# Projections of q and k as f32r products of high and low parts, in place of fp32 products, in an attention and experts kernel

## What is computed

```python
q = _split_heads(x @ Wq.T + bq); k = _split_heads(x @ Wk.T + bk); v = _split_heads(x @ Wv.T + bv)
q = jnp.exp(q); k = jnp.exp(k)
kv = jnp.cumsum(k[:, :, :, None] * v[:, :, None, :], axis=1)
k1 = jnp.cumsum(k, axis=1)
out = einsum('zsD,zsDd->zsd', q, kv) / sum(q * k1, -1)      # then @ Wo.T + bo
x = layernorm(x + attention)
scores = sigmoid(x @ gate_w.T)                               # routing: top 2 of 4 groups, top 8 experts
outs = silu(x @ expert_gate) * (x @ expert_up) @ expert_down # weighted by the router, plus the shared expert
x = layernorm(x + experts)
```

## Time and profile before

| | |
|---|---|
| runs, us | 462.74, 462.77, 463.14 (median 462.77) |
| the profiled execution, us | 463.29 |
| its span, us | 461.5 |
| busy share of the span | TensorE 92%, VectorE 75%, GpSimd 61%, ScalarE 59% |
| mean granted TensorE clock | 0.970 |

### The profile page before, as it was taken

The page is one execution under the profiler, slowest core; times in us unless marked ns, Lnnn a source line. Parts: engine busy times, 40 slices in busy tenths (PEclk is TensorE's granted clock), DMA queues, the critical chain, the costliest instruction groups (busy, mean ns, idle before and its releaser), DMA issues.

```text
span 461.5 us, 10791 instructions
## 1 busy us (share of the span) xinstructions
PE 424.0 (92%) x3954; PEld 324.8 (70%) x3954; DVE 347.4 (75%) x909; ACT 273.3 (59%) x530; POOL 282.4 (61%) x208
## 2 busy tenths in 40 slices
PE   5855799999999999999999999999999999899982
PEld 3733587778867787778877787778877787578761
DVE  2678548797878968797878968796878968777652
ACT  3835334963587546963587546963587546555642
POOL 2565236864676557864677557764677557757781
PEclk9989589999999999999999999999999999999996
DMA  7400544346440823446340923446440913466500
GB/s 233 187 1 1 147 92 90 92 97 141 93 113 7 197 69 82 91 103 135 91 116 12 202 68 74 90 104 134 91 116 9 200 41 81 91 134 129 121 11 23
DMA packets 28660, 45.08 MB, mean 98 GB/s; under 512 B 1984, under 2 KB 10304, under 8 KB 28224
## 3 DMA queue, kind: packets, MB, share of 16 engines
q1 hardware_dynamic: 28608, 44.40, 41.2%
HBM read 41.77 MB, written 2.62 MB: 96 GB/s over the span
## 4 chain that ended last, share of the span: by engine, by line
PE 40%; DVE 32%; issue 12%; POOL 8%; ACT 2%; DVEq 1%; ACTq 0%; POOLq 0%
PE bank L326 39%; DVE units L866 7%; POOL units L958 5%; DVE stats L741 2%; DVE hidden_lo L721 2%; POOL rstd L977 2%; DVE top_of_group L782 2%; DVE x L753 2%; DVE bank L775 1%; ACT hidden_hi L584 1%; DVE replaced L814 1%; DVE out_sb L878 1%; DVE k_sum L847 1%; DVE probs L731 1%; DVE kv_blocks L836 1%
## 5 line engine op out<-in xcount | busy, mean ns | idle before, releaser
L958 POOL TENSOR_TENSOR units<-units,weight_wide 128x512 f32<-128x512 f32 x128 | 174.3, 1367 | 130.5 <-DVE units L866 115.9
L602 ACT ACTIVATE units<-bank 128x512 f32<-128x512 f32 x136 | 80.7, 594 | 79.2 <-PE bank L326 78.9
L866 DVE TENSOR_TENSOR units<-bank,units 128x512 f32<-128x512 f32 x136 | 92.9, 683 | 35.1 <-PE bank L326 28.0
L584 ACT ACTIVATE hidden_hi<-units 128x512 fp32r<-128x512 f32 x136 | 86.1, 634 | 53.7 <-POOL units L958 47.7
L721 DVE TENSOR_TENSOR hidden_lo<-units,hidden_hi 128x512 fp32r<-128x512 f32 x112 | 97.7, 873 | 19.6 <-ACT hidden_hi L584 18.8
L326 PE MATMUL bank<-x_hi,gate_hi 128*128 128x512 f32 x136 | 62.1, 457 | 2.0 <-DVE units L866 1.6
L326 PE MATMUL bank<-hidden_hi,down_hi 128*128 128x512 f32 x136 | 55.0, 404 | 1.7 <-DVE hidden_lo L721 1.7
L326 PE MATMUL bank<-x_hi,up_hi 128*128 128x512 f32 x136 | 54.7, 403 | 1.8 <-ACT units L602 1.8
L326 PE MATMUL bank<-x_lo,gate_hi 128*128 128x512 f32 x136 | 54.6, 401 | 0.0
L326 PE MATMUL bank<-x_hi,gate_lo 128*128 128x512 f32 x136 | 54.4, 400 | 0.0
L326 PE MATMUL bank<-x_hi,up_lo 128*128 128x512 f32 x136 | 54.1, 398 | 0.0
(11 more groups left out here) (107 smaller groups left out, 670.8 us busy)
## 6 DMA issues: line engine op xcount, KB each, us to landing
weight_wide<-weight_d SPq DMA_DIRECT2D x62, 512.0 KB, 6.7
xT<-xT_in SPq DMA_DIRECT2D x8, 256.0 KB, 6.8
x_tok<-x_in SPq DMA_DIRECT2D x8, 256.0 KB, 6.9
out_dram<-out_sb SPq DMA_DIRECT2D x8, 256.0 KB, 2.3
weight_wide<-up_in SPq DMA_DIRECT2D x1, 1088.0 KB, 9.0
up_raw<-up_in SPq DMA_DIRECT2D x1, 1088.0 KB, 11.0
down_raw<-down_in SPq DMA_DIRECT2D x1, 1088.0 KB, 13.2
weight_d<-weightT SPq DMA_DIRECT2D x8, 64.0 KB, 1.6
```

The lines of the kernel that those rows point to most:

```text
L584: nc.scalar.activation(hidden_hi[place(n, g)][:, :], units[place(n, g)][:, :], ACT.Copy).then_inc(hidden_hi_done, 1)
L602: nc.scalar.activation(units[place(n, g)][:, :], up_banks[2 * n % 3][:, :], ACT.Silu).then_inc(silu_done, 1)
L866: V.tensor_tensor(units[place(n, g)][:, :], up_banks[(2 * n + 1) % 3][:, :], units[place(n, g)][:, :], ALU.mult).then_inc(gated_done, 1)
L958: G.tensor_tensor(units[place(n, g)][:, :], units[place(n, g)][:, :], weight_wide[:, (n - 1) % (2 * PIECE), :], ALU.mult).then_inc(hidden_ ...
```

## The change

For groups two to seven the projections of k and q become three f32r products each. Groups zero and one keep the fp32 products. The weights of q and k, 256 columns, are split once, in g = 0: ScalarE copies the high part in slot 6, GpSimd subtracts for the low part in slot 7. The activations `xT` are split once a group: ScalarE copies `xT_hi` at the end of slot 8, GpSimd subtracts for `xT_lo` in slot 9, behind unit 9 and ahead of `x1_lo`. TensorE waits for both before the product of k. The v projection stays fp32 and reads `xT` itself.

```diff
--- before.py
+++ after.py
@@ -69,6 +69,8 @@
         up_lo = sb("up_lo", [128, BLOCKS * 128], F32R)
         down_hi = sb("down_hi", [128, BLOCKS * 128], F32R)
         down_lo = sb("down_lo", [128, BLOCKS * 128], F32R)
+        wqk_hi, wqk_lo = (sb(name, [128, 2 * DIM], F32R) for name in ("wqk_hi", "wqk_lo"))
+        xT_hi, xT_lo = (sb(name, [128, GROUP], F32R) for name in ("xT_hi", "xT_lo"))
         neg_half = sb("neg_half", [128, TILES])
 
 
@@ -159,6 +161,7 @@
         gate_loaded, up_loaded, down_loaded, gate_split, up_split, down_split, setup_chain = (
             sem(n) for n in ("gate_loaded", "up_loaded", "down_loaded", "gate_split", "up_split", "down_split", "setup_chain"))
         bias_mm, bias_done, xT_loaded, q_proj = (sem(n) for n in ("bias_mm", "bias_done", "xT_loaded", "q_proj"))
+        wqk_split, xT_hi_done, xT_lo_done = (sem(n) for n in ("wqk_split", "xT_hi_done", "xT_lo_done"))
         q_exp, k_proj, k_exp, q_masked, first_masked = (
             sem(n) for n in ("q_exp", "k_proj", "k_exp", "q_masked", "first_masked"))
         v_proj, v_copied, v_spread, kT_turned = (sem(n) for n in ("v_proj", "v_copied", "v_spread", "kT_turned"))
@@ -409,6 +412,14 @@
                                       start=False, stop=pair == 1, skip_group_check=True)
                 if b == SEQS - 1:
                     last.then_inc(o_ready, 1)
+
+            def projection(f, bank, w, cols):
+
+                if f < 2:
+                    return mm(bank[:, :], w, xT[:, :])
+                mm(bank[:, :], wqk_hi[:, cols], xT_hi[:, :], stop=False)
+                mm(bank[:, :], wqk_hi[:, cols], xT_lo[:, :], start=False, stop=False)
+                return mm(bank[:, :], wqk_lo[:, cols], xT_hi[:, :], start=False)
 
             def turn_exponentials(m):
 
@@ -497,12 +508,17 @@
 
                     pe.wait_ge(attn_done, reached(f))
                     pe.wait_ge(xT_loaded, reached(16 * (f + 1)))
-                    mm(o_bank[:, :], wkT, xT[:, :]).then_inc(k_proj, 1)
+                    if f == 2:
+                        pe.wait_ge(wqk_split, 2)
+                    if f > 1:
+                        pe.wait_ge(xT_hi_done, f - 1)
+                        pe.wait_ge(xT_lo_done, f - 1)
+                    projection(f, o_bank, wkT, slice(DIM, 2 * DIM)).then_inc(k_proj, 1)
                     pe.wait_ge(resid2_done, reached(f - 1))
                     pe.wait_ge(kv_copied, reached(SEQS * f))
                     if f == 1:
                         pe.wait_ge(inv_copied, 1)
-                    mm(work_bank[:, :], wqT, xT[:, :]).then_inc(q_proj, 1)
+                    projection(f, work_bank, wqT, slice(0, DIM)).then_inc(q_proj, 1)
                     if mid:
                         turn_exponentials(m)
                 if front and n == 11:
@@ -698,6 +714,12 @@
                 if g == -1 and mid and n == 5:
                     act.wait_ge(down_loaded, 16)
                     nc.scalar.activation(down_hi[:, :], down_raw, ACT.Copy).then_inc(down_split, 1)
+                if g == 0 and n == 6:
+                    nc.scalar.activation(wqk_hi[:, :], attn_w[:, 0:2 * DIM], ACT.Copy).then_inc(wqk_split, 1)
+                if front and f > 1 and n == 8:
+                    act.wait_ge(xT_loaded, 16 * (f + 1))
+                    act.wait_ge(q_proj, f)
+                    nc.scalar.activation(xT_hi[:, :], xT[:, :], ACT.Copy).then_inc(xT_hi_done, 1)
 
             schedule(slot)
 
@@ -975,6 +997,13 @@
                     pool.wait_ge(var1_done, reached(m + 1))
                     pool.wait_ge(x1_done, reached(m))
                     G.tensor_tensor(rstd1[:, :], var1[:, :], neg_half[:, :], ALU.pow).then_inc(rstd1_done, 1)
+                if g == 0 and n == 7:
+                    pool.wait_ge(wqk_split, 1)
+                    G.tensor_tensor(wqk_lo[:, :], attn_w[:, 0:2 * DIM], wqk_hi[:, :].bitcast(F32), ALU.subtract
+                                    ).then_inc(wqk_split, 1)
+                if front and f > 1 and n == 9:
+                    pool.wait_ge(xT_hi_done, f - 1)
+                    G.tensor_tensor(xT_lo[:, :], xT[:, :], xT_hi[:, :].bitcast(F32), ALU.subtract).then_inc(xT_lo_done, 1)
                 if mid and n == 9:
                     pool.wait_ge(x1T_copied, reached(m + 1))
                     pool.wait_ge(x1_hi_done, reached(m + 1))
```

## The result

The changed kernel took 478.98 us, median of 4 runs (477.00 to 481.53), against 462.95 us of the kernel before on the same chip: 1.034 times as long, 95% interval 1.030 to 1.038. The direction and the wait came out as told, the granted clock did not; the time is 4.8 us over the forecast and 1.0 us outside the range. The profiled execution took 480.62 us with a span of 478.8 us, 17.3 more than before.

The account below looks back on a forecast made before the run. The prediction took the moment of exp_negT's transposition, held by exp_negT, as the bound. Waits of 9.2 and 1.67 us plus 0.6 for the weights made 11.5 us on a 461.5 us span; forecast 474.2 us, range 469.5 to 478.

Parts of the forecast that it names:

- The direction: Whole kernel: slower by more than 0.2%, given a chance of 94%.
- the range: Whole kernel's time: 469.5 to 478 us, about 8 in 10, leaving out a fall of the clock.
- The bound: Each group: the start of exp_negT's transposition on TensorE moves VectorE's router and all that follows by the same amount.
- The gain of the f32r products, 0: k and q projections: at most 0.34 us saved in six groups, none reaching the transposition, which waits for exp_negT.
- the first after an idle stretch: TensorE's projections: the first f32r product after idling takes 0.34 us, so six take 1.49 us after a wait.
- The wait for xT_lo, 1.84 us in five groups, 1.67 in g = 0: TensorE before the k product: GpSimd's late subtraction delays the transposition by 1.84 us, 1.67 in g = 0.
- the copy's shift of the silu: ScalarE, end of slot 8: copying xT_hi holds the engine 0.54 us, making GpSimd's unit 9 end 0.17 us later.
- two hand-overs: Unit 9's gated product to GpSimd, 0.04 us, and xT_lo's end to TensorE's products, 0.05 us.
- The split of the weights, 0.6 us: Once in g = 0: GpSimd's 0.75 us subtraction holds off VectorE's, putting 0.6 us into the chain (0 to 0.75).
- The lock between GpSimd and VectorE: GpSimd's subtractions: a VectorE instruction with two SBUF inputs excludes GpSimd; the first to start holds off the other.
- The clock: TensorE at the projections: idling drops it to 1.2 GHz, fifteen slow products, 3.0 us a group, 492 us; chance 5%.
- The sum: Whole span: 9.2 + 1.67 + 0.6 = 11.5 us on 461.5, so 473.0; profiled execution 474.8, forecast 474.2 us.

Follow-up runs that it names:

- e8_turn_first: The changed kernel with the transposition of exp_negT put ahead of the projections on TensorE: 475.90 us, 1.0272 of the kernel before.
- e1_early: The changed kernel with the split of xT (ScalarE's copy and GpSimd's subtraction) moved forward to slot 4: 464.08 us, 1.0014 of the kernel before.
- e5: The kernel before with ScalarE's silu of unit 10 put ahead of the high part of unit 8: 462.99 us, 0.9997 of the kernel before.
- e6: The changed kernel with xT split in slot 4, ScalarE's silu of unit 10 ahead of unit 8's high part, weights split in slot 3: 460.85 us, 0.9952.
- e9_ahead: The changed kernel with xT_lo ahead of unit 9's multiply on GpSimd and ScalarE's copy in slot 4: 464.63 us, 1.0031 of the kernel before.
- after: The changed kernel itself, in its first measurement beside the kernel before: 478.98 us, 1.034 of the kernel before.
- after_again: The changed kernel, unchanged, measured a second time beside the kernel before: 480.50 us, 1.0367 of the kernel before.
- e2: The changed kernel with all splits and waits kept, but fp32 products of k and q: 480.11 us, 1.0375 of the kernel before.
- e4: The changed kernel with only ScalarE's copy xT_hi moved forward to slot 4: 479.43 us, 1.0345 of the kernel before.
- e3: The changed kernel with seven useless f32r products put ahead of TensorE's wait for xT_hi and xT_lo: 489.15 us, 1.0570 of the kernel before.
- e7: The changed kernel with xT_lo behind x1_lo on GpSimd instead of ahead of it: 489.33 us, 1.0572 of the kernel before.

## Why the prediction was right in kind and too low in size

Step by step:

- **The bound.** Right: the start of the transposition moves, and the periods move with it. It was not the router alone, though: e8_turn_first shows that TensorE's stream is as tight, so there was no room on either side.
- **The gain of the f32r products, 0.** Right (e1_early). The 0.34 us for "the first after an idle stretch" was misread, since TensorE had not been idle before 132.18; behind a real idle stretch it was 0.31 (137.65 to 137.96), and the six took 1.46 us for 1.49. e5 and e6 show why: two things ended within 0.1 us.
- **The wait for xT_lo, 1.84 us in five groups, 1.67 in g = 0.** The mechanism and its place were right; 2.06 and 1.73 were measured where the clock stood. `xT_lo` itself was right to the digit (1.71 for 1.71), the copy's shift of the silu too (0.52 for 0.54). Too low were two hand-overs: I had the gated product's end to GpSimd's unit 9 at 0.04 us and it is 0.15 (134.40 to 134.55), and `xT_lo`'s end to TensorE at 0.05 and it is 0.15 (137.50 to 137.65). The 0.05 came from a hand-over of ScalarE to TensorE; for the 0.04 the prediction names no row. In the trace of the kernel before, VectorE's gated products reached a waiting GpSimd after 0.08 us in 56 of 72 cases and after 0.14 or 0.15 in 16. Five times 0.22 and 0.06 are 1.2 us.
- **The split of the weights, 0.6 us.** Right in detail. `wqk_lo` took 0.75 us and held off VectorE's subtraction, which ended at 78.57 where I had 78.60:

```profile
77.27 0.75 POOL L1002 TENSOR_TENSOR wqk_lo<-attn_w,wqk_hi 128x256 fp32r<-128x256 f32 x1
```

```profile
77.36 1.21 DVE L743 TENSOR_TENSOR hidden_lo<-units,hidden_hi 128x512 fp32r<-128x512 f32 x1
```

- **The lock between GpSimd and VectorE.** What I drew from the Trainium skill (SBUF — State Buffer, Who interferes with whom) agrees with the rows of all the kernels. Where two subtractions on GpSimd follow unit 9, the first takes 1.71 to 1.77 us and the next 1.25 to 1.29; in e9_ahead, in the groups with projections, it is unit 9 itself that meets VectorE's subtraction and takes 1.74, and both subtractions on GpSimd take 1.27 to 1.30. And here GpSimd came first and VectorE's 0.68 us became 1.21.
- **The clock: the step that failed.** I gave the fall a 5% chance, on one row: no fall after 1.60 us idle in g = 6. It fell in three of the six groups, and cost there 1.05, 1.16 and 1.23 us over the undisturbed 6.61, 3.4 us together. One row without a fall was taken for a rule. The same trace had falls to weigh against it: early in the run the granted clock goes to 0.50 at 31.1 and at 44.7, each at most 1.4 us behind the end of an idle stretch of some 3 us:

```profile
29.70 0.66 PE L493 MATMUL bank<-const,x 128*128 128x128 f32 x4 [3.29 <-DVE x L753]
44.04 0.61 PE L541 MATMUL bank<-const,weight 128*32 128x128 f32 x4 [3.00 <-DVE weight L823]
```

```profile
31.00:34.40 3.40, 2.96 (x19) 2.41 (x19) 3.40 (x2) 1.23 (x4) 3.40 (x2) 0.51 0.02 5
44.60:61.70 17.10, 13.33 (x218) 10.41 (x218) 8.72 (x14) 4.86 (x13) 2.54 (x2) 0.50 0.65 150
```

  Nor was my price right: 3.0 us a group for fifteen slow products. The 0.20 us for each held, but only seven to nine were slow, six of them ahead of L427.
- **The sum.** Of the 17.3 us of span: 12.0 are the wait (1.73 + 5 x 2.06), 3.4 the clock at the products, 0.5 the weights. Of the last 1.4 us, 0.7 are lost in the last 70 us, and they are clock too: at the end of the run the granted clock falls once more, in the kernel before at 454.3, when TensorE has done its last product, and in the changed kernel at 467.9, ahead of its last five. The last four, which transpose `yT`, in the kernel before and in the changed one:

```profile
452.63 0.63 PE L446 MATMUL bank<-const,yT 128*128 128x128 f32 x4 [0.78 <-ACT yT L593]
```

```profile
469.53 1.08 PE L457 MATMUL bank<-const,yT 128*128 128x128 f32 x4 [0.78 <-ACT yT L609]
```

  In all twelve profiled executions the time from the transposition of `exp_negT` in g = 6 to the end goes by this: 67.9 to 68.0 us where the last fall comes 61 to 63 us behind that transposition, 68.5 to 69.1 where it comes 57 to 58 us behind it. The other 0.6 to 0.7 us lie spread over the periods, and their cause is open. The profiled execution took 480.6 us where I had 474.8: 4.1 of the 5.8 us are clock, 1.1 my terms (12.5 for 11.5), the rest is open. Without its three falls at the products it would be at 477.2 us, and two of the four executions lie there, at 477.00 and 477.34 with a mean granted clock of 0.965 and 0.966 against 0.957; they were not profiled, so that they had no such fall is inferred. So the waits alone would have stayed inside the range, and the falls took the median out of it; the range had left the clock out.

The Trainium skill (TensorE: Matmul & The Clock Gate, The HAM clock gate), which has the clock fall after idling, was the rival to weigh higher. The runs agree with it in kind; but the clock fell here behind shorter idle stretches than that page would let one expect, and there the measurement decides. The profiled executions by the length of the idle stretch:

- 1.24 and 1.25 us in g = 6 (e5, e6): no fall in 2 places
- 1.34 to 1.57 ahead of L427 in the groups with projections (e8): 1 fall in 6
- 1.57 to 1.60 in g = 6: 3 in 10
- 1.76 to 1.86 at the products (after, after_again, e2, e4): 11 in 24, all of them in g = 2 to 5 and none in the 8 places of g = 0 and 1
- the stops of e3: none behind 0.70 to 1.79, a fall behind 2.13 and behind 2.20
- 2.99 to 3.06 (e7): 5 in 6
- e1, e5, e6 and e9, with no idle stretch over 0.7 us in the groups with projections: none there

On the whole the longer idle stretches had more falls. What decides in one group and not in the next at the same idle length is open.

## What to carry to other kernels

Before a product is made cheaper by splitting its operands, ask when the engines that make the parts get to them: here the change cost sixteen microseconds with one part behind an instruction of GpSimd, and one to two with it ahead. Where two things end together at a hand-over, shortening one was worth nothing, and both together what each had promised. An idle stretch on TensorE has two prices, itself and the clock, and a single row without a fall is no evidence that the second is nil.

## What the runs showed of the hardware

- Idle stretches of 1.3 to 1.9 us on TensorE were followed by half clock in some groups and not in others, at the same length to 0.02 us; each fall at the products cost 0.95 to 1.23 us in the changed kernel (both measurements), 0.3 to 0.9 in e4_copy_early and 1.7 in e2_fp32_wait.
- Seven products more a group, in time in which TensorE had nothing to do, brought stops of 0.7 to 2.2 us some 33 us later that the profile calls "issue", and each stop ended 2.4 to 2.6 us behind the start of a 16 KB packet of the queue named "instruction" (e3_filler). More instructions on TensorE were not free even in idle time.
- The hand-overs to a waiting engine, from the releaser's end to the start, have two lengths in the kernel before: from VectorE's gated product to GpSimd 0.08 us in 56 cases and 0.14 or 0.15 in 16, from ScalarE to TensorE 0.05 in 5 and 0.14 in 4. From GpSimd to TensorE, which only the changed kernels have, it was 0.14 or 0.15 each time. What makes a hand-over the longer one is open.
